# Moving the low parts of the directly read blocks of S from VectorE to GpSimd in a graph-and-experts kernel

## The chip, the core and the metric

The kernel runs on one core of one Trainium2 chip. The metric is the device time of one execution in microseconds. In the profile PE is TensorE's matmul, PEld its weight load, DVE VectorE, ACT ScalarE, POOL GpSimd, and SP SyncE, which issues most of the transfers.

## The reference

Input are `x` (8, 2048, 128), an adjacency matrix `adj` (2048, 2048) and the weights. All is float32.

```
# graph layer
HW    = layernorm(x) @ W
A     = relu((adj + adj.T) / 2);  d = rowsum(A) ** -0.5
x1    = x + relu((I - d A d) @ HW)            # S is the matrix of this product
# mixture of 8 experts, top 2 of each token
t     = layernorm(x1)
gates = normalised top 2 of softmax(t @ router_w.T)
out   = x1 + t + sum over e of gates[e] * (gelu(t @ w1[e] + b1[e]) @ w2[e] + b2[e])
```

## The kernel before, in words

**The matrix.** S is symmetric, and the scale d on both sides is put into the other operand and into the result. So the kernel keeps only one triangle of 128x128 blocks, 136 of them, in the tile `s_tri`. To be exact enough each operand of a matmul is split into a high part (rounded to fp32r) and a low part (the rest), and a product takes three matmuls: high by high, high by low and low by high (lines 969, 970, 971).

**Units.** The batches go in two halves of four. A half has 16 units, one for each block of 128 nodes, and a unit is 16 steps of three 128x512 matmuls into one PSUM bank. Units 0 to 15 (the first half) go from node block 15 down to 0, units 16 to 31 from 0 up to 15. For unit u of the first half the column of S for node block n = 15 - u is made ready in one of two `stage` tiles, high and low parts side by side. Its blocks n to 15, u + 1 of them, are read straight from the triangle: `high_direct` (ACT, line 432) copies them, `low_direct` (line 437) subtracts the copy. The other n blocks have to be turned on PE, in groups of four, into PSUM: `turn_group` (line 446), `high_group` (ACT, line 453), `low_group` (DVE, line 460). The second half loads the columns back from memory, where SP's `store_stage` (line 858) has put them; the triangle's place is then taken by `y1`, the second half's operand.

**One iteration.** The loops of all engines in the graph stage run over the same u. While PE multiplies unit u, the others finish unit u - 1 and make the stage of unit u + 1. The order on each engine is written out by hand:
- PE: 16 steps of unit u. Before the first it waits for the stage's low parts. Between the steps it does the turns, at step 4 `route(u - 2)` (line 919, the router's product, which waits for `z_lo_done`), at steps 6 and 9 the two projections of x for the second half (line 342, units 8 to 15 only), at step 12 `turn_z(u - 1)` (line 906).
- ACT: `evict(u - 1)` (line 984, it starts when unit u - 1 has left PE), `high_direct(u + 1)`, then copies and groups, `copy_z(u - 1)` (line 991).
- DVE: `mid(u - 1)` (lines 1065 to 1075: residual, statistics, `var_eps`), `low_direct(u + 1)`, then in four slots the low groups, `scale` of the two projections (line 367, each waits for its projection), in two units of four a part of the routing (`pick` in u = 5, 9, 13, from line 1087; `share` in u = 6, 10, 14, from line 1129), and `low` of the two projections (line 379). Then the statistics of the next two x tiles (line 284, which wait for their transfer), `diagonal(u + 2)` (line 422) and `z_low(u - 1)` (line 1079).
- POOL: `finish_unit(u - 1)`: `rstd` by a power (line 1033, it waits for `var_eps`), z in four pieces (line 1038), the residual `res` (line 1043). For u = 7 to 14 then the power for the next two projections (line 296) and their scale (line 316).
- SP: `store_stage(u)`, the load of the residual's x, the loads of two x tiles (line 270), `store_unit(u - 1)`, which waits for `res` and for `z_low(u - 1)`.

After unit 31 the experts follow: 256 rounds of up and down products on PE, with GELU on ACT and the gates on DVE.

One semaphore, `lo_made`, counts all low parts, direct and turned, in the order in which DVE makes them; `ops_before` and `ops_with` translate a unit or a group into that count.

Of the kernel before, what the change touches and what calls it, by code (L numbers as in the profile page):

```python
# [4 lines left out]
FP32 = mybir.dt.float32  # L5
FP32R = mybir.dt.float32r
ALU = mybir.AluOpType
# [222 lines left out]
def project_program(nc, sem, v):  # L230
# [3 lines left out]
    Q, CW, MB = v.Q, v.CW, v.MB  # L234
# [123 lines left out]
    def scale(dve, k):  # L358

        _, m = place(k)  # L360
        staged = MB - 1 - (128 - 8 * m) // 17
        dve.wait_ge(v.st.hi_made, v.st.ops_before[staged + 1])
        dve.wait_ge(v.st.s_turned, v.st.groups_before[staged + 1])
        dve.wait_ge(v.st.lo_made, v.st.ops_before[staged + 1])
        dve.wait_ge(hw_done, k + 1)
        dve.wait_ge(y_scale_done, m + 1)
        dve.tensor_tensor(out=v.y1_whole[m][:, :].rearrange("p (q f) -> p q f", f=P),
                          in0=ps_p[k][:, :].rearrange("p (q f) -> p q f", f=P),
                          in1=v.y_scale[:, m, :, None].to_broadcast([P, Q, P]), op=ALU.mult).then_inc(y1_made, 1)
# [18 lines left out]
def stage_program(nc, sem, v):  # L388


    MB, Q = v.MB, v.Q
    ps_t = [v.banks[2], v.banks[3]]
    st = Plan()
    diag_done = sem("diag_done")
    st.s_turned = s_turned = sem("s_turned")
    st.hi_made = hi_made = sem("hi_made")
    st.lo_made = lo_made = sem("lo_made")
    st.acc_done = sem("acc_done")
    st.stage_out = [sem(f"stage_out{i}") for i in range(2)]

    def column(u):
        return MB - 1 - u

    def n_groups(u):
        return (column(u) + Q - 1) // Q

    st.groups_before = [sum(n_groups(i) for i in range(u)) for u in range(MB + 1)]
    st.ops_before = [u + st.groups_before[u] for u in range(MB + 1)]

    ops_with = [st.ops_before[u] + 2 + g for u in range(MB) for g in range(n_groups(u))]  # L410

    def direct(u):
        n = column(u)
        if n < 8:
            return v.s_tri[:, 17 * n:16 * n + 16, :]
        return v.s_tri[:, 17 * n - 120:16 * 15 + n - 120 + 1:16, :]

    def diagonal(dve, u):
        n = column(u)
        dve.wait_ge(v.deg_step, v.deg_steps_until(n))  # L420
        b = block(n, n)
        dve.scalar_tensor_tensor(out=v.s_tri[:, b, :], in0=v.ident[:, :], scalar=v.deg_neg[:, n:n + 1],
                                 in1=v.s_tri[:, b, :], op0=ALU.mult, op1=ALU.add).then_inc(diag_done, 1)

    def high_direct(act, u):
        n = column(u)
        act.wait_ge(diag_done, u + 1)
        if u == 1:
            act.wait_ge(v.summed, v.all_groups)
        wait(act, st.acc_done, u - 1)  # L430
        wait(act, st.stage_out[u % 2], 16 * (u // 2))
        act.activation(v.stage[u % 2][:, 0, n:MB, :], direct(u), ACT.Copy).then_inc(hi_made, 1)

    def low_direct(dve, u):
        n = column(u)
        dve.wait_ge(hi_made, st.ops_before[u] + 1)
        dve.tensor_tensor(out=v.stage[u % 2][:, 1, n:MB, :], in0=direct(u),
                          in1=v.stage[u % 2][:, 0, n:MB, :].bitcast(FP32), op=ALU.subtract).then_inc(lo_made, 1)

    def turn_group(pe, u, g):  # L440
        n, G = column(u), st.groups_before[u] + g
        if G >= 2:
            pe.wait_ge(lo_made, ops_with[G - 2])
        for m in range(Q * g, min(Q * g + Q, n)):
            i = m - Q * g
            last = pe.transpose(ps_t[G % 2][:, i * P:(i + 1) * P], v.s_tri[:, block(n, m), :], v.ident[:, :])  # L446
        last.then_inc(s_turned, 1)

    def high_group(act, u, g):
        n, G = column(u), st.groups_before[u] + g  # L450
        a, b = Q * g, min(Q * g + Q, n)
        act.wait_ge(s_turned, G + 1)
        act.activation(v.stage[u % 2][:, 0, a:b, :].rearrange("p m f -> p (m f)"), ps_t[G % 2][:, 0:(b - a) * P],
                       ACT.Copy).then_inc(hi_made, 1)

    def low_group(dve, u, g):
        n, G = column(u), st.groups_before[u] + g
        a, b = Q * g, min(Q * g + Q, n)
        dve.wait_ge(hi_made, ops_with[G])
        dve.tensor_tensor(out=v.stage[u % 2][:, 1, a:b, :].rearrange("p m f -> p (m f)"),  # L460
                          in0=ps_t[G % 2][:, 0:(b - a) * P],
                          in1=v.stage[u % 2][:, 0, a:b, :].rearrange("p m f -> p (m f)").bitcast(FP32),
                          op=ALU.subtract).then_inc(lo_made, 1)

    st.n_groups, st.diagonal, st.high_direct, st.low_direct = n_groups, diagonal, high_direct, low_direct
    st.turn_group, st.high_group, st.low_group = turn_group, high_group, low_group
    return st

# [315 lines left out]
def graph_stage(nc, sem, v):  # L784
    B, E, MB, CW, Q, U, T = v.B, v.E, v.MB, v.CW, v.Q, v.U, v.T
    ident, pr, st = v.ident, v.pr, v.st
# [47 lines left out]
    def jobs(u):  # L834
        return [MB + 2 * (u - 8), MB + 2 * (u - 8) + 1] if 8 <= u < MB else []
# [18 lines left out]

    def sync(sp):
        def store_stage(u):
            sp.wait_ge(st.lo_made, st.ops_before[u + 1])
            sp.dma_start(v.s_dram[node_block(u)], v.stage[u % 2][:, :, :, :].bitcast(FP32)).then_inc(st.stage_out[u % 2], 16)

        def load_stage(n):  # L860
            s = (n + 1) % 2
            sp.wait_ge(acc_done, MB + n - 1)
            if n == 2:
                for i in range(2):
                    sp.wait_ge(st.stage_out[i], 16 * 7)
            sp.dma_start(v.stage[s][:, :, :, :].bitcast(FP32), v.s_dram[n]).then_inc(stage_in[s], 16)

        def load_x(u):
            wait(sp, x1_done, u)
            sp.dma_start(v.x_res[:, :, :], v.x_units[half(u), node_block(u)]).then_inc(x_res_in, 16)  # L870

        def store_unit(u):
            sp.wait_ge(res_done, u + 1)
            sp.dma_start(v.res_dram[unit(u)], v.res[:, :, :].rearrange("p q f -> p (q f)")).then_inc(res_out[half(u)], 16)
            sp.wait_ge(z_hi_done, u + 1)
            sp.wait_ge(z_lo_done, u + 1)
            sp.dma_start(v.z_dram[unit(u)], v.z_hl[:, :, :].bitcast(FP32)).then_inc(z_out[half(u)], 16)

        v.store_unit, v.store_gates = store_unit, store_gates
        sp.wait_ge(v.summed, v.all_groups)  # L880
        for u in range(U):
            if MB < u + 1 < U and node_block(u + 1) >= 2:
                load_stage(node_block(u + 1))
            if u < MB - 2:
                store_stage(u)
            load_x(u)
            for k in jobs(u + 1):
                pr.load(sp, k)
            if u == MB + 4:
                sp.wait_ge(acc_done, MB)  # L890
                v.load_weights(sp)
            if u == MB + 7:
                v.place_b2_low(sp)
            if u >= 7 and u % 4 == 3:
                store_gates(sp, (u - 7) // 4)
            if u == U - 2:
                v.load_first(sp)
            if u:
                store_unit(u - 1)

    def tensor(pe):
# [47 lines left out]
        for u in range(U):  # L949
            h = half(u)  # L950
            if h == 0:
                s = u % 2
                pe.wait_ge(st.lo_made, st.ops_before[u + 1])
                order = range(MB - 1, -1, -1)
            else:
                s = (u + 1) % 2
                if node_block(u) >= 2:
                    pe.wait_ge(stage_in[s], 16 * (node_block(u) // 2))
                order = range(MB)
            wait(pe, evicted, u - 1)  # L960
            out = acc[u % 2]
# [68 lines left out]
    def gpsimd(pool):  # L1030
# [16 lines left out]
        for u in range(U):  # L1047
            if u:
                finish_unit(u - 1)
            if jobs(u + 1):  # L1050
                pr.invert(pool, jobs(u + 1))
                for k in jobs(u + 1):
                    pr.scale_by_d(pool, k)
            if u == MB + 4:
                pool.wait_ge(acc_done, MB)
                v.zero_rows(pool)
            if u == MB + 5:
                v.weights_low(pool)
        finish_unit(U - 1)

    def vector(dve):
# [110 lines left out]
        def share(batch):  # L1172
# [7 lines left out]
                          op=ALU.subtract).then_inc(router_lo, 1)  # L1180
        for u in range(U):
            ahead = u + 1 < MB
            ks = jobs(u)
            if u:
                mid(u - 1)
            if ahead and u:
                st.low_direct(dve, u + 1)
            for g in range(4):
                if u and ahead and g < st.n_groups(u + 1):
                    st.low_group(dve, u + 1, g)  # L1190
# [317 lines left out]
```

## Time and profile before

| | |
|---|---|
| median of 3 runs | 901.16 us (900.66, 901.16, 905.78) |
| profiled execution | 904.51 us, of which span 902.8 us |
| PE, PEld busy | 854.5 us, 712.1 us |
| DVE busy | 637.2 us |
| ACT busy | 479.7 us |
| POOL busy | 297.9 us |
| granted clock of TensorE, mean | 0.983 of full speed |

The span is cut by the stages so: setup to about 87 us, the first half's units from there to about 324 us (unit 8 is reached at 193 us), the second half's units to about 520 us, and the experts. In a list of instructions each line gives start and duration in us, the engine, the line of the kernel, the operation with what it writes and reads, the shapes and how many were merged into the line, and in square brackets how long the engine had been idle before it and which engine, tile and line released it.

### The profile page before, as it was taken

How to read it: one execution, taken by the hardware profiler on the slowest of the kernel's cores; microseconds unless marked ns; L12 is line 12 of the kernel's file. 1: busy time of each engine (PE TensorE's matmuls, PEld its weight loads, DVE VectorE, ACT ScalarE, POOL GpSimd, SP SyncE). 2: the span in 40 equal slices, each digit the busy share in tenths (PEclk: the TensorE clock that was granted, in tenths of full speed). 3: DMA queues.
4: the chain of work that ended last, by engine and by line, in shares of the span. 5: the costliest groups of instructions: out<-in, count | busy, mean ns of one | idle time of the engine just before them, and what ended most of it. 6: DMA issues, size and time to landing. Idle time of an engine off the chain costs nothing.

```text
span 902.8 us, 14486 instructions
## 1 busy us (share of the span) xinstructions
PE 854.5 (95%) x4146; PEld 712.1 (79%) x4146; DVE 637.2 (71%) x1552; ACT 479.7 (53%) x872; POOL 297.9 (33%) x312
## 2 busy tenths in 40 slices
PE   4788999999899899999999999999999999999996
PEld 3688788888777788878888776888888888888884
DVE  3676644757867735262626388999999999999995
ACT  2686423233333211111011378888888888888885
POOL 1794243563564544574444440010000000000001
PEclk9896999999999999999999999999999999999999
DMA  9993366685675337877777856667777777777771
GB/s 287 315 308 122 122 261 234 227 291 191 208 260 194 111 113 264 313 258 287 278 286 267 311 219 262 260 259 284 280 268 271 275 282 274 273 272 281 283 283 46
DMA packets 93006, 222.98 MB, mean 247 GB/s; under 512 B 8888, under 2 KB 59600, under 8 KB 81056
## 3 DMA queue, kind: packets, MB, share of 16 engines
q1 hardware_dynamic: 87760, 212.96, 66.4%
q0 software_dynamic: 2688, 8.59, 2.4%
q10 hardware_dynamic: 2512, 0.86, 0.4%
q8 instruction: 23, 0.38, 0.2%
q14 instruction: 23, 0.19, 0.1%
HBM read 157.89 MB, written 64.49 MB: 246 GB/s over the span
## 4 chain that ended last, share of the span: by engine, by line
PE 69%; issue 9%; POOL 9%; DVE 6%; DMA 3%; ACT 2%; DVEq 0%; SPq 0%; ACTq 0%; POOLq 0%
PE bank L969 8%; PE bank L971 8%; PE bank L970 8%; PE bank L1379 6%; PE bank L1363 6%; PE bank L1365 6%; PE bank L1364 6%; PE bank L1376 6%; PE bank L1377 6%; POOL z L1038 5%; PE bank L342 3%; DMA x_raw<-in_x 2%; POOL rstd L1033 2%; PE bank L446 2%; PE bank L1385 1%
## 5 line engine op out<-in xcount | busy, mean ns | idle before, releaser
L1415 ACT ACTIVATE act_h<-bank,b_sb 128x512 f32<-128x512 f32 x256 | 176.6, 690 | 48.1 <-PE bank L1365 44.9
L1453 DVE TENSOR_TENSOR gated<-c_all,act_h 128x512 f32<-128x512 f32 x256 | 176.5, 690 | 30.8 <-ACT act_h L1415 25.0
L1458 DVE TENSOR_TENSOR g_lo<-gated,g_hi 128x512 fp32r<-128x512 f32 x256 | 175.7, 686 | 0.2
L1422 ACT ACTIVATE g_hi<-gated 128x512 fp32r<-128x512 f32 x256 | 159.4, 623 | 4.5 <-DVE gated L1453 4.5
L1346 POOL DMA_DIRECT2D out<-fin x32 | 24.3, 760 | 344.3 <-DVE fin L1466 333.2
L1038 POOL TENSOR_SCALAR z<-x,mv,rstd 128x128 f32<-128x128 f32 x128 | 106.4, 846 | 3.4
L969 PE MATMUL bank<-y_hi,stage 128*128 128x512 f32 x256 | 105.7, 413 | 0.7 <-DVE y_lo L743 0.7
L1363 PE MATMUL bank<-z_e,w_hi 128*128 128x512 f32 x256 | 102.8, 402 | 2.5 <-ACT act_h L1415 2.5
L991 ACT ACTIVATE z_hl<-bank 128x512 fp32r<-128x512 f32 x32 | 19.1, 598 | 157.2 <-PE bank L906 157.2
L1379 PE MATMUL bank<-g_lo,w_hi 128*128 128x512 f32 x256 | 100.9, 394 | 1.4 <-DVE g_lo L1458 1.3
L971 PE MATMUL bank<-y_hi,stage 128*128 128x512 f32 x256 | 101.4, 396 | 0.0
L969 PE MATMUL bank<-y,stage 128*128 128x512 f32 x256 | 101.2, 395 | 0.0
L1033 POOL TENSOR_TENSOR rstd<-var_eps,neg_half 128x4 f32<-128x4 f32 x32 | 48.8, 1526 | 158.5 <-DVE var_eps L1075 158.5
L970 PE MATMUL bank<-y_lo,stage 128*128 128x512 f32 x256 | 101.0, 394 | 0.0
L1376 PE MATMUL bank<-g_hi,w_lo 128*128 128x512 f32 x256 | 100.0, 391 | 0.0
L1365 PE MATMUL bank<-z_e,w_lo 128*128 128x512 f32 x256 | 99.9, 390 | 0.0
L971 PE MATMUL bank<-y,stage 128*128 128x512 f32 x256 | 99.9, 390 | 0.0
L1364 PE MATMUL bank<-z_e,w_hi 128*128 128x512 f32 x256 | 99.8, 390 | 0.0
L1377 PE MATMUL bank<-g_hi,w_hi 128*128 128x512 f32 x256 | 99.7, 389 | 0.0
L970 PE MATMUL bank<-y,stage 128*128 128x512 f32 x256 | 99.7, 389 | 0.0
L1079 DVE TENSOR_TENSOR z_hl<-bank,z_hl 128x512 fp32r<-128x512 f32 x32 | 22.0, 688 | 72.3 <-ACT z_hl L991 72.3
L1379 PEld LDWEIGHTS bank<-g_lo,w_hi 128*128 128x128 f32 x256 | 48.0, 188 | 14.9 <-DVE g_lo L1458 5.1
(128 smaller groups left out, 1481.9 us busy)
## 6 DMA issues: line engine op xcount, KB each, us to landing
c_all<-c_scratch SPq DMA_DIRECT2D x64, 1024.0 KB, 8.2
s_scratch<-stage SPq DMA_DIRECT2D x14, 2048.0 KB, 8.5
stage<-s_scratch SPq DMA_DIRECT2D x14, 2048.0 KB, 7.8
z_e<-z_scratch SPq DMA_DIRECT2D x32, 512.0 KB, 7.0
z_scratch<-z_hl SPq DMA_DIRECT2D x31, 512.0 KB, 2.7
x_raw<-in_x SPq DMA_DIRECT2D x32, 256.0 KB, 7.7
x_res<-in_x SPq DMA_DIRECT2D x32, 256.0 KB, 7.1
r_e<-res_scratch SPq DMA_DIRECT2D x32, 256.0 KB, 2.7
```

The source lines that it names most:

```text
L969: pe.matmul(out[:, :], s_hi, y_hi, start=(i == 0), stop=False)
L970: pe.matmul(out[:, :], s_hi, y_lo, start=False, stop=False)
L971: last = pe.matmul(out[:, :], s_lo, y_hi, start=False, stop=(i == MB - 1))
L1363: pe.matmul(ps_h[k][:, :], v.w1_hi[:, e, :], v.z_e[s][:, 0, :], start=True, stop=False)
L1364: pe.matmul(ps_h[k][:, :], v.w1_hi[:, e, :], v.z_e[s][:, 1, :], start=False, stop=False)
L1365: pe.matmul(ps_h[k][:, :], v.w1_lo[:, e, :], v.z_e[s][:, 0, :], start=False, stop=True).then_inc(h_done, 1)
L1376: pe.matmul(ps_o[s][:, :], v.w2_lo[:, e, :], hi[:, :], start=False, stop=False)
L1379: pe.matmul(ps_o[s][:, :], v.w2_hi[:, e, :], lo[:, :], start=False, stop=(e == E - 1)).then_inc(o_done, 1)
L1415: act.activation(v.act_h[e % R][:, :], ps_h[e % 2][:, :], ACT.Gelu, bias=v.b1_sb[:, e:e + 1]).then_inc(gelu_done, 1)
L1422: act.activation(v.g_hi[e % R][:, :], v.gated[e % R][:, :], ACT.Copy).then_inc(hi_done, 1)
L1453: dve.tensor_tensor(out=v.gated[e % R][:, :], in0=v.c_all[s][:, e, :], in1=v.act_h[e % R][:, :], op=ALU.mult).then_inc(gated_done, 1)
L1458: dve.tensor_tensor(out=v.g_lo[e % R][:, :], in0=v.gated[e % R][:, :], in1=v.g_hi[e % R][:, :].bitcast(FP32), op=ALU.subtract).then_inc(lo ...
```

## The change

`low_direct` of units 2 to 15 is taken off DVE's list in the graph stage and put on POOL's, behind `finish_unit(u - 1)` and ahead of the power for the projections. Those of units 0 and 1 stay on DVE in the setup. The direct low parts get a semaphore of their own, `direct_lo`, and `lo_made` now counts the turned groups alone; PE, SP and DVE wait for both where they waited for one.

```diff
-        dve.wait_ge(v.st.lo_made, v.st.ops_before[staged + 1])
+        dve.wait_ge(v.st.direct_lo, staged + 1)
+        dve.wait_ge(v.st.lo_made, v.st.groups_before[staged + 1])
...
-    def low_direct(dve, u):
+    def low_direct(eng, u):
         n = column(u)
-        dve.wait_ge(hi_made, st.ops_before[u] + 1)
-        dve.tensor_tensor(out=v.stage[u % 2][:, 1, n:MB, :], in0=direct(u),
-                          in1=v.stage[u % 2][:, 0, n:MB, :].bitcast(FP32), op=ALU.subtract).then_inc(lo_made, 1)
+        eng.wait_ge(hi_made, st.ops_before[u] + 1)
+        eng.tensor_tensor(out=v.stage[u % 2][:, 1, n:MB, :], in0=direct(u),
+                          in1=v.stage[u % 2][:, 0, n:MB, :].bitcast(FP32), op=ALU.subtract).then_inc(direct_lo, 1)
...
         if G >= 2:
-            pe.wait_ge(lo_made, ops_with[G - 2])
+            pe.wait_ge(lo_made, G - 1)
...
         def store_stage(u):
-            sp.wait_ge(st.lo_made, st.ops_before[u + 1])
+            sp.wait_ge(st.direct_lo, u + 1)
+            sp.wait_ge(st.lo_made, st.groups_before[u + 1])
...
             if h == 0:
                 s = u % 2
-                pe.wait_ge(st.lo_made, st.ops_before[u + 1])
+                pe.wait_ge(st.direct_lo, u + 1)
+                pe.wait_ge(st.lo_made, st.groups_before[u + 1])
...
         for u in range(U):                       # POOL
             if u:
                 finish_unit(u - 1)
+            if u and u + 1 < MB:
+                st.low_direct(pool, u + 1)
             if jobs(u + 1):
                 pr.invert(pool, jobs(u + 1))
...
             if u:                                # DVE
                 mid(u - 1)
-            if ahead and u:
-                st.low_direct(dve, u + 1)
             for g in range(4):
```

## Rows read from the trace of the kernel before

**Rows 1.** From the page: busy time, share and instructions of each engine.

```profile
PE 854.5 (95%) x4146; PEld 712.1 (79%) x4146; DVE 637.2 (71%) x1552; ACT 479.7 (53%) x872; POOL 297.9 (33%) x312
```

**Rows 2.** PE's waits, 100 to 330 us: waiter, releaser, us in total, times, longest.

```profile
PE bank L919 <- issue: 4.8, 2, 3.0
PE bank L919 <- DVE z_hl L1079: 3.6, 3, 1.4
```

**Rows 3.** DVE's instructions in order of time, iterations 9 to 14.

```profile
219.43 0.29 DVE L1089 TENSOR_TENSOR logits<-gate_parts 128x128 f32<-128x128 f32 x1
...
235.26 0.69 DVE L367 TENSOR_TENSOR y_whole<-bank,y_scale 128x512 f32<-128x512 f32 x1 [1.70 <-PE bank L342]
...
236.41 0.28 DVE L1134 TENSOR_TENSOR picked<-expo,same 128x128 f32<-128x128 f32 x1
...
237.04 0.86 DVE L1142 SCALAR_TENSOR_TENSOR guarded<-sum_all,sum_top 128x16 f32<-128x16 f32 x1
...
257.66 0.87 DVE L284 BATCH_NORM_STATS2 x_stats<-x_raw 128x6 f32<-128x128 f32 x4 [3.79 <-DMA x_raw<-in_x]
...
268.85 1.56 DVE L379 TENSOR_TENSOR y<-y_whole,y 128x512 fp32r<-128x512 f32 x2
272.22 0.87 DVE L284 BATCH_NORM_STATS2 x_stats<-x_raw 128x6 f32<-128x128 f32 x4 [1.81 <-DMA x_raw<-in_x]
...
275.65 0.69 DVE L1079 TENSOR_TENSOR z_hl<-bank,z_hl 128x512 fp32r<-128x512 f32 x1
...
284.72 0.29 DVE L1089 TENSOR_TENSOR logits<-gate_parts 128x128 f32<-128x128 f32 x1
...
285.37 0.93 DVE L1106 TENSOR_TENSOR shifted<-logits,top 128x128 f32<-128x128 f32 x1
...
303.39 1.10 DVE L1129 TENSOR_TENSOR same<-is_1st,is_2nd 128x128 f32<-128x128 f32 x1
```

**Rows 4.** All direct low parts of DVE: count, ns least/median/most, first and last start.

```profile
L437 DVE TENSOR_TENSOR stage<-s_tri,stage x16: 292/1285/2282, 76.0 to 296.5; 128x128 fp32r<-128x128 f32 x1, 128x256 fp32r<-128x256 f32 x1, 128x384 fp32r<-128x384 f32 x1, 128x512 fp32r<-128x512 f32 x1
```

**Rows 5.** POOL's instructions in order of time, iterations 9, 10, 12, 13, 14 and 16.

```profile
211.11 2.34 POOL L1033 TENSOR_TENSOR rstd<-var_eps,neg_half 128x4 f32<-128x4 f32 x1 [0.63 <-DVE var_eps L1075]
...
230.78 2.47 POOL L1033 TENSOR_TENSOR rstd<-var_eps,neg_half 128x4 f32<-128x4 f32 x1 [0.62 <-DVE var_eps L1075]
...
236.58 1.28 POOL L1043 TENSOR_TENSOR res<-x,z 128x512 f32<-128x512 f32 x1
...
263.72 2.74 POOL L1033 TENSOR_TENSOR rstd<-var_eps,neg_half 128x4 f32<-128x4 f32 x1 [0.62 <-DVE var_eps L1075]
...
278.58 2.87 POOL L1033 TENSOR_TENSOR rstd<-var_eps,neg_half 128x4 f32<-128x4 f32 x1 [0.62 <-DVE var_eps L1075]
...
296.72 3.00 POOL L1033 TENSOR_TENSOR rstd<-var_eps,neg_half 128x4 f32<-128x4 f32 x1 [0.62 <-DVE var_eps L1075]
...
326.93 1.03 POOL L1033 TENSOR_TENSOR rstd<-var_eps,neg_half 128x4 f32<-128x4 f32 x1 [7.00 <-DVE var_eps L1075]
```

**Rows 6.** POOL's two-operand instructions in the setup, by form: busy, mean ns, idle before.

```profile
L573 POOL TENSOR_TENSOR col_sum<-col_sum,s_tri 128x1024 f32<-128x1024 f32 x6 | 14.2, 2368 | 2.0 <-ACT s_tri L608 2.0
...
L573 POOL TENSOR_TENSOR col_sum<-col_sum,s_tri 128x640 f32<-128x640 f32 x2 | 3.1, 1548 | 0.0
```

**Rows 7.** A long POOL instruction and DVE beside it, iteration 21.

```profile
393.82 5.21 POOL L1275 TENSOR_TENSOR w_lo<-w_raw,w_hi 128x1024 fp32r<-128x1024 f32 x2 [2.09 <-ACT w_hi L1262]
...
395.49 1.29 DVE L1065 TENSOR_TENSOR x<-x,x_res 128x512 f32<-128x512 f32 x1 [2.09 <-ACT x L984]
```

**Rows 8.** ACT and PE in iteration 13: unit 12 has left PE; the router's product.

```profile
273.73 0.69 ACT L984 ACTIVATE x<-bank,d_out 128x512 f32<-128x512 f32 x1 [2.17 <-PE bank L971]
...
276.83 0.40 PE L919 MATMUL bank<-z_hl,router 128*128 128x512 f32 x1
```

**Rows 9.** Two stretches after PE's long waits: busy times, then PEclk, DMA share, GB/s.

```profile
230.00:235.00 5.00, 5.00 (x34) 4.48 (x33) 3.45 (x9) 1.66 (x3) 4.26 (x5) 1.00 1.12 427
...
295.00:299.00 4.00, 4.00 (x17) 3.45 (x16) 3.68 (x11) 1.30 (x2) 3.27 (x4) 0.57 0.87 262
```

More of the change, by code:

```diff
@@ L396, in stage_program @@
     st.hi_made = hi_made = sem("hi_made")
+    st.direct_lo = direct_lo = sem("direct_lo")
     st.lo_made = lo_made = sem("lo_made")
```

## The prediction

> **What bounds the kernel now.** I read the page first. PE is busy for 95% of the span [rows 1], so the change can gain only where PE stands still, and loses wherever it makes PE stand longer. Next come PE's own waits in the first half. All but one of those that matter are in front of one instruction, the router's product at step 4 of iterations 10, 11, 12, 14 and 15: 4.8 us in two waits and 3.6 us in three, 8.4 us together [rows 2]. It waits for `z_low`, the last thing on DVE's list of the iteration before. So DVE's list sets the pace from iteration 9 on, though DVE is idle 29% of the span. In the order of time one sees what the list itself waits for: for the second projection (1.70 us idle in iteration 10), and in iterations 11 and 12 for the x tiles' transfer (3.79 and 1.81 us); in 10, 13 and 14, which carry a routing part, it runs from the second `scale` to `z_low` with no such wait [rows 3]. Anything put into that last stretch reaches PE in full.
>
> **What is removed.** 14 subtractions of DVE, up to 2282 ns each [rows 4]. They stand between `var_eps` and the first `scale`. The second `scale` waits for a projection that PE reaches at step 9, whatever DVE did before, and DVE already idles 1.70 us there [rows 3]. So taking the 1.75 us subtraction away in iteration 10 makes that wait longer and nothing earlier. I take a gain of 0 on DVE; the cover is PE's five steps from `route` to the second projection. POOL does gain: its power `rstd` takes 1.03 us alone, and 2.34 to 3.00 us where DVE's subtraction runs beside it [rows 5]. z comes 1.3 to 2 us sooner; PE hardly waits for z, so this is worth 0 too. But it decides where the new instruction lands.
>
> **What is added.** A two-operand POOL instruction takes 2368 ns for 1024 elements and 1548 ns for 640 [rows 6], so 2.14 ns an element and 0.18 us besides, 0.273 us a block: 3.2 us for unit 10 (11 blocks), 3.5, 3.7, 4.0, 4.3 and 4.55 us for unit 15 (16 blocks), about twice DVE's own. It starts behind `res`. In iteration 10 the power ends at 230.78 + 2.47 = 233.25 and `res` at 237.86, 4.61 us later; with the power at 1.03 us, `res` ends 1.03 + 4.61 = 5.64 us after the power's start and the new instruction begins 0.06 us later, so at start + 5.70.
>
> Is it late for PE? In iteration 12 it is there from 263.72 + 5.70 = 269.42 to about 273.9 (with one short hold by DVE), and unit 12 leaves PE at 273.73 [rows 5, 8]. Unit 13 would begin about 0.2 us late, and the wait at `route` swallows that. The others come out earlier or as close. What is queued behind it on POOL, the next power, waits for x statistics that end later still: 0. SP stores the stage only after `z_low`, later than that: 0. The added waits of PE, SP and DVE are on counts already reached: 0. Units 2 to 8 have small subtractions and a DVE with slack: 0.
>
> **The port.** Here is the real cost. `L1142`, 16 elements wide, starts at 237.04 beside POOL's `res` and takes 0.86 us: it ends at 237.90, and `res` at 237.86 [rows 3, 5]. `L1106` takes 0.93 us and `L1129` 1.10 us beside a `res`, where `L1089` on the same shape takes 0.29 [rows 3]. Beside a longer one, `w_lo` of 2.6 us, a residual addition of 512 elements takes 1.29 us, where `L367` of that size takes 0.69: it gets in only between the two instructions [rows 3, 7]. So a DVE instruction with two operands in SBUF stands until POOL's ends, also when POOL's is long. The Trainium skill says the same (SBUF — State Buffer, section Who interferes with whom: a DVE instruction with two SBUF inputs and a GpSimd one that reads SBUF exclude each other, for the whole instruction). By it the sum below stands; without it only the first rival's 0 to 3 us would be left.
>
> **The sum**, in the times of before (what comes later shifts as a whole). Iteration 9: the new instruction runs from 211.11 + 5.70 = 216.8 to 220.0; `L1089` wants to start at 219.43 and ends 0.7 us later than before. Iteration 10: DVE's `L1129`, waiting since before `res` ended, is let in first, then the new instruction runs from about 236.6 to 240.1. `L1134` (236.41, end 236.69) now ends at 240.2, which is +3.5; the 0.7 us that `L1142` loses to `res` is saved: +2.8. Iteration 11: the pair `L379` is held, but 3.79 us of idle time behind it cover that: +0.1. Iteration 12: of the pair at 268.85 the second is held until 273.9 and ends at 274.45, 2.2 us past the 272.22 at which the statistics began; these had a second wait of 0.2 us inside, so 2.0 remain. `z_low` ended at 276.34 and `route` began at 276.83, so PE loses 1.5, but POOL and DVE 2.0, and the next iteration's hold hangs on POOL: +2.0. Iteration 13: 278.58 + 5.70 + 4.3 = 288.6; `L1089` (284.72) ends 3.75 us later; `L1106` saves 0.64: +3.1. Iteration 14: 296.72 + 5.70 + 4.55 = 307.0; `L1129` ended at 304.49, now at 307.1: +2.6 [rows 3, 5, 8].
>
> That is 11.3 us. Then the clock. After PE's wait of 3.0 us the granted clock is 0.57 over 4 us, close to the lower of its two levels (1.2 GHz), which costs 0.43 x 4 = 1.7 us; after the other long wait, 1.8 us, it is 1.00 [rows 2, 9]. The waits in iterations 11 and 15 grow past 3 us (1.2 on average, plus 2.8 and 2.6). In 11 the transfer's wait covers the loss. In 15 nothing does: +1.7. Sum 13.0 us. The profiled execution would go from 904.5 to 917.5 us. It lies 0.4% above the median of the runs shown; from 901.2 the forecast is **914 us**.
>
> Bounds. POOL's price in the form with an fp32r output is 5.21 / 2 = 2.6 us per 1024 at most, against 2.37 [rows 6, 7]; 10% on the six is +2 us. Further clock drops in iterations 10 and 13 cost at most 1.7 us each: 919 to 920. Below: if DVE's second `L379` slips in ahead of POOL in iteration 12, that iteration costs 0.8 at most, and if the clock does not drop in 15, 1.7 less: 911.
>
> **Rivals.**
> *The port hardly counts* (DVE gets in between pieces of POOL's long instruction). For it: no row shows a POOL instruction of 4 us with DVE beside it. Against: the 2.6 us one held DVE. Then only lateness at the unit starts and a power of 1.03 us remain: 901 to 904 us. Chance 0.18.
> *The gain on DVE counts.* Of the six subtractions 11.7 us (1.62 to 2.28) leave DVE; if `z_low` followed that, PE's 8.4 us of waits would go and with them the clock drop of 1.7: 891 us. It decides if the second `scale` is not held by PE, and the 1.70 us idle says it is. Chance 0.08.
> *POOL becomes the bound at the unit starts.* If the subtraction takes 10 to 15% more and DVE's short instructions get in ahead of it, units 12 to 15 start 0.5 to 1.2 us late each, and longer PE waits drop the clock after four units: 914 + 4 + 2 x 1.7 = 921 us and up to 925. Chance 0.12.
> The forecast has 0.62.
>
> **How the numbers follow.** 1%, 9 us, is about what a measurement of this kernel can tell from no change. Faster by more: 0.07, nearly all of the second rival. Within 1%: the first rival, a bit of the second, and the part of the forecast's own case in which the holds are shorter (below 910): 0.25. Slower: 0.68. The forecast's own range is 909 to 919. To leave out no more than 2 in 10 it must reach the first rival's upper part and the third's middle: 903 to 921.
>
> **What would show it.** Right: L437 on POOL with 3.2 to 4.6 us in iterations 9 to 14; `L1089` or `L1129` and `L1134` in 10, 13 and 14 with durations of 3 to 4 us, ending with it; `rstd` near 1.03 us; PE's waits at the router's product up from 8.4 to near 20 us; and low clock behind two or more of them. Wrong: short durations of those DVE instructions; a second `scale` that starts sooner; PE waiting at line 969 for POOL.

## The result: 916.8 us, 1.6% slower

The changed kernel took 916.83 us in the median of four runs (916.57 to 917.65), the kernel before 901.62 in four. The ratio is 1.0158, 95% interval 1.0128 to 1.0188. The profiled execution took 917.65 us with a span of 916.0, which is 13.2 us over the span of before. The forecast was 914 on the median and +13.0 in the profiled execution.

### The profile page after: what moved, and what is told of

It is laid out like the page before. It is cut to its first block, busy times and chain, and to the rows that moved or that the text cites. A ratio compares the mean times of both kernels' runs of the same rounds, so it can differ in the third digit from the quotient of the medians.

```text
span 916.0 us, 14517 instructions
## 1 busy us (share of the span) xinstructions
PE 856.8 (94%) x4146; PEld 712.0 (78%) x4146; DVE 637.4 (70%) x1538; ACT 479.1 (52%) x872; POOL 320.9 (35%) x326
## 4 chain that ended last, share of the span: by engine, by line
PE 66%; issue 10%; POOL 9%; DVE 8%; ACT 4%; DMA 2%; DVEq 0%; SPq 0%; ACTq 0%; POOLq 0%
PE bank L973 7%; PE bank L975 7%; PE bank L974 7%; PE bank L1383 5%; PE bank L1367 5%; PE bank L1369 5%; PE bank L1368 5%; PE bank L1380 5%; PE bank L1381 5%; POOL z L1042 5%; PE bank L342 3%; PE bank L448 2%; POOL res L1047 2%; ACT s_tri L610 1%; PE bank L1389 1%
## 5 line engine op out<-in xcount | busy, mean ns | idle before, releaser
L1037 POOL TENSOR_TENSOR rstd<-var_eps,neg_half 128x4 f32<-128x4 f32 x32 | 33.4, 1043 | 153.5 <-DVE var_eps L1081 153.5
```

## The profile after

Lines of the kernel have moved: 437 is 439, 919 is 922, 969 is 973, 1033 is 1037, 1079 is 1085, 1089 is 1095, 1129 is 1135, 379 is 380. In the experiments they move by a few more; the tile's name tells which instruction is meant. First the page's line of busy times, against [rows 1].

```profile
PE 856.8 (94%) x4146; PEld 712.0 (78%) x4146; DVE 637.4 (70%) x1538; ACT 479.1 (52%) x872; POOL 320.9 (35%) x326
```

DVE has 14 instructions fewer and is as busy as before. The work that left it came back as waiting: an instruction held by POOL counts as busy from its start. So a share of busy time does not show this loss. PE's waits of the first half (100 to 345 us) do, against [rows 2].

```profile
PE bank L922 <- issue: 8.3, 2, 5.5
PE bank L922 <- DVE z_hl L1085: 8.0, 4, 4.0
PE bank L973 <- POOL stage L439: 1.4, 3, 0.6
```

The waits at the router's product have gone from 8.4 to 16.3 us. POOL's own lateness at the start of a unit costs PE 1.4 us in three waits. Next POOL in order of time, against [rows 5].

```profile
211.32 1.04 POOL L1037 TENSOR_TENSOR rstd<-var_eps,neg_half 128x4 f32<-128x4 f32 x1 [0.63 <-DVE var_eps L1081]
...
216.93 3.22 POOL L439 TENSOR_TENSOR stage<-s_tri,stage 128x1408 fp32r<-128x1408 f32 x1
...
236.96 3.50 POOL L439 TENSOR_TENSOR stage<-s_tri,stage 128x1536 fp32r<-128x1536 f32 x1
...
272.64 4.48 POOL L439 TENSOR_TENSOR stage<-s_tri,stage 128x1792 fp32r<-128x1792 f32 x1
...
289.26 4.34 POOL L439 TENSOR_TENSOR stage<-s_tri,stage 128x1920 fp32r<-128x1920 f32 x1
...
310.40 4.61 POOL L439 TENSOR_TENSOR stage<-s_tri,stage 128x2048 fp32r<-128x2048 f32 x1
```

The power takes 1.04 us where it took 2.34, and the subtraction what the setup's sums had told: 3.2, 3.5, 4.0, 4.3 and 4.55 expected. The one of 1792 elements has some wait inside. DVE in order of time, against [rows 3]: the instructions that were held, and all of `z_low` from iteration 8 to 14.

```profile
208.39 0.68 DVE L1085 TENSOR_TENSOR z_hl<-bank,z_hl 128x512 fp32r<-128x512 f32 x1
...
219.06 1.24 DVE L1095 TENSOR_TENSOR logits<-gate_parts 128x128 f32<-128x128 f32 x1
...
228.43 0.68 DVE L1085 TENSOR_TENSOR z_hl<-bank,z_hl 128x512 fp32r<-128x512 f32 x1
...
237.43 0.69 DVE L368 TENSOR_TENSOR y_whole<-bank,y_scale 128x512 f32<-128x512 f32 x1 [2.93 <-PE bank L342]
238.04 2.58 DVE L1135 TENSOR_TENSOR same<-is_1st,is_2nd 128x128 f32<-128x128 f32 x1
...
247.74 0.68 DVE L1085 TENSOR_TENSOR z_hl<-bank,z_hl 128x512 fp32r<-128x512 f32 x1
...
255.80 5.26 DVE L380 TENSOR_TENSOR y<-y_whole,y 128x512 fp32r<-128x512 f32 x2
...
264.10 0.68 DVE L1085 TENSOR_TENSOR z_hl<-bank,z_hl 128x512 fp32r<-128x512 f32 x1
...
272.14 5.54 DVE L380 TENSOR_TENSOR y<-y_whole,y 128x512 fp32r<-128x512 f32 x2
...
280.71 0.68 DVE L1085 TENSOR_TENSOR z_hl<-bank,z_hl 128x512 fp32r<-128x512 f32 x1
...
289.51 4.23 DVE L1095 TENSOR_TENSOR logits<-gate_parts 128x128 f32<-128x128 f32 x1
...
301.88 0.68 DVE L1085 TENSOR_TENSOR z_hl<-bank,z_hl 128x512 fp32r<-128x512 f32 x1
...
311.23 3.93 DVE L1135 TENSOR_TENSOR same<-is_1st,is_2nd 128x128 f32<-128x128 f32 x1
...
322.01 0.68 DVE L1085 TENSOR_TENSOR z_hl<-bank,z_hl 128x512 fp32r<-128x512 f32 x1
```

An instruction of 128 elements takes 4.23 us. It starts at 289.51, 0.25 us behind POOL's, and ends at 293.74; POOL's ends at 293.60. The same 0.29 us instruction was [rows 3]'s line at 284.72. The starts of `z_low` give the account by iteration:

| iteration | before | after | lag | gained in it | forecast |
|---|---|---|---|---|---|
| 8 | 208.17 | 208.39 | 0.22 | | |
| 9 | 227.85 | 228.43 | 0.58 | +0.4 | +0.7 |
| 10 | 244.34 | 247.74 | 3.40 | +2.8 | +2.8 |
| 11 | 260.79 | 264.10 | 3.31 | -0.1 | +0.1 |
| 12 | 275.65 | 280.71 | 5.06 | +1.8 | +2.0 |
| 13 | 293.79 | 301.88 | 8.09 | +3.0 | +3.1 |
| 14 | 311.35 | 322.01 | 10.66 | +2.6 | +2.6 |

Last PE and ACT: three stretches of the changed kernel behind PE's waits of 2.83, 5.50 and 4.00 us (iterations 10, 14, 15), against [rows 9], and the moment at which unit 15 has left PE.

```profile
229.20:235.00 5.80, 5.79 (x24) 5.14 (x25) 3.22 (x12) 2.52 (x5) 4.96 (x8) 0.71 0.89 362
...
302.60:308.00 5.40, 5.34 (x24) 4.58 (x25) 2.67 (x11) 2.33 (x4) 4.57 (x7) 0.72 0.67 197
322.80:328.00 5.20, 5.16 (x22) 4.42 (x23) 2.37 (x11) 0.22 (x1) 4.63 (x7) 0.68 0.58 189
```

```profile
336.02 0.69 ACT L988 ACTIVATE x<-bank,d_out 128x512 f32<-128x512 f32 x1 [2.17 <-PE bank L975]
```

The same eviction was at 323.88 before: 12.1 us of lag, 1.5 more than `z_low` had in iteration 14. The low clock of iteration 15, (1 - 0.68) x 5.2 = 1.7 us, accounts for that. The lag stays at 12.1 us through the second half. The last 1.0 us comes in the experts, 0.7 of it in one step where PE waits 0.5 us for the load of `z_e`; nothing ties it to the change.

## The experiments

Each ratio is to the kernel before, timed together with that run; absolute times of different experiments compare less well.

**e1 and e2: early units alone, late units alone.**

```diff
-            if u and u + 1 < MB:                 # e1
+            if u and u + 1 <= 8:
                 st.low_direct(pool, u + 1)
...
+            if ahead and u + 1 >= 9:
+                dve.wait_ge(st.direct_lo, u + 1)
+                st.low_direct(dve, u + 1)
...
-            if u and u + 1 < MB:                 # e2
+            if u + 1 >= 10 and u + 1 < MB:
                 st.low_direct(pool, u + 1)
...
+            if u and u + 1 <= 9:
+                st.low_direct(dve, u + 1)
```

> Only the direct low parts of units 2 to 8 are on POOL, those of 9 to 15 are back on DVE. Port theory (a long POOL subtraction holds DVE's two-operand instructions, `z_low` comes late, PE waits for it at the router's product): in iterations 1 to 7 DVE has slack before `z_low`, so 901 to 903 us, no change from before. If the added waits or the second count cost something, or POOL's lateness in general, part of the 15 us stays: 904 to 908.

> Only units 10 to 15 are on POOL (iterations 9 to 14), units 2 to 9 are back on DVE. Port theory: all of the loss is here, 914 to 917 us. A loss spread over all units by their size (133 blocks, 81 of them in these six) would give 61% of it: 910 to 911.

e1: 903.17 us against 903.88, ratio 0.9996 (0.9981 to 1.0010). e2: 917.94 us, ratio 1.0160 (1.0127 to 1.0193). All of the loss that shows lies in the six late iterations. The second count with its waits, and POOL's work in the early units, cost nothing that can be told from 0. A loss that follows the blocks handled would have shown 1.0096 in e2.

**e3: POOL's instruction cut to one block.**

```diff
+        end = MB if u < 2 else n + 1
...
-        eng.tensor_tensor(out=v.stage[u % 2][:, 1, n:MB, :], in0=direct(u),
+        eng.tensor_tensor(out=v.stage[u % 2][:, 1, n:end, :], in0=direct(u)[:, 0:end - n, :],
...
```

> As the change, but POOL's subtraction covers only the first block (0.46 us); the other direct low parts are left out. Nothing is on DVE in their place. Port theory with no gain on DVE: the holds fall to 0.3 us, PE's waits at the router's product go back to about 8 us: 900 to 903 us. If DVE's relief is worth something once POOL is out of the way: 891 to 897.

900.95 us, ratio 0.9978 (0.9957 to 1.0000). With the order of the change but without its length the loss is gone. And this bounds DVE's relief: taking all 14 subtractions off DVE, with POOL out of the way, is worth 2 us, with 0 to 4 in the interval, and not 10. PE's waits at the router's product are those of before:

```profile
PE bank L923 <- issue: 4.3, 2, 2.4
PE bank L923 <- DVE z_hl L1086: 3.3, 3, 1.6
```

The second `scale` of iteration 10 shows where the relief goes:

```profile
231.74 0.69 DVE L368 TENSOR_TENSOR y_whole<-bank,y_scale 128x512 f32<-128x512 f32 x1 [2.72 <-PE bank L342]
```

It starts 7.40 us after the iteration's `z_low` began (224.34), and in the kernel before 7.41 us after (227.85 to 235.26) [rows 3]. The 1.75 us that DVE no longer spends became idle time, 1.0 us here and 0.55 us in front of the first `scale`.

**e4: a subtraction that nobody waits for, added to the kernel before.**

```diff
...
+            if u and u + 1 < MB:
+                k = min(u + 2, 11)
+                each = v.ident[:, None, :].to_broadcast([P, k, P])
+                pool.tensor_tensor(out=v.spare[:, 0:k, :], in0=each, in1=each, op=ALU.subtract)
```

> The kernel before, with DVE's subtraction where it was, and beside it a POOL subtraction of constants into unused memory behind `finish_unit`, of u + 2 blocks at most 11 (3.2 us); no instruction waits for it. Port theory: it starts 1.3 to 2 us later than in the changed kernel, behind the slower power, and then holds DVE in iteration 9 for 1.7 us, in 10 for 2.7, in 13 and 14 for 3 each, in 11 and 12 for nothing: 10 us and a clock drop or two, 911 to 914 us. If the loss is POOL's lateness for PE: 901 to 902, since nothing waits for this one.

915.73 us against 903.88, ratio 1.0133 (1.0102 to 1.0164). That is 12 us, what was expected (10 us and a clock drop or two), though the absolute time lies above the range given. Nothing waits for this instruction, yet it costs most of what the change cost. So the cost of the change is for the most part not when POOL's result comes, but what POOL keeps from DVE meanwhile. POOL and DVE of iteration 13:

```profile
293.61 2.59 POOL L1054 TENSOR_TENSOR spare<-ident 128x1408 fp32r<-128x1408 f32 x1
```

```profile
293.73 2.62 DVE L1113 TENSOR_TENSOR same<-logits,top 128x128 f32<-128x128 f32 x1
```

Both end within 0.15 us of each other. My durations were off: this form takes 2.6 us and not 3.2, so the holds are shorter. From iteration 8 to 14 `z_low` falls back by 9.2 us against the kernel before (210.99 to 323.33, there 208.17 to 311.35). Behind PE's waits (15.8 us together) the clock is low in four iterations, with a mean of 0.72 over 6 us in three of them.

**e5 and e6: `z_low` ahead of the x statistics**, in the kernel before and in the changed one.

```diff
+            if u:
+                z_low(u - 1)
             for k in jobs(u + 1):
                 pr.statistics(dve, k)
             if u + 2 < MB:
                 st.diagonal(dve, u + 2)
-            if u:
-                z_low(u - 1)
```

> The kernel before with `z_low` ahead of the x statistics and the diagonal on DVE's list, nothing else. If z_low's place at the end of the list is what hands DVE's lateness to PE, PE's 8 us at the router's product go, and the 1.7 us of low clock behind them; part comes back as waits at other places (for z at step 12, for the x tiles' transfer): 893 to 897 us. If PE's wait only moves: 900 to 904.

> The changed kernel with the same edit. The port theory says that POOL's holds of 3 to 4 us lie ahead of `z_low` in either order, so they still make it late, but 3 us of statistics no longer come on top: PE waits where hold is longer than that, about 2 us each in iterations 13 and 14 and the starts of units 12 to 14 are late by 0.5 us each: 900 to 906 us. If the 15 us came from something else than z_low's lateness, 912 or more.

e5: 904.06 us, ratio 1.0020 (1.0005 to 1.0035). e6: 919.57 us, ratio 1.0189 (1.0164 to 1.0215). Both expectations failed. PE's waits of e5, 100 to 345 us:

```profile
PE bank L342 <- ACT x_t L329: 6.9, 3, 3.4
```

and of e6:

```profile
PE bank L342 <- ACT x_t L329: 11.6, 5, 3.4
```

In e5 the wait at the router's product is gone and stands at step 6; in e6 most of it has moved there. `diagonal` is still behind the statistics; ACT's `high_direct` waits for it, and on ACT the x copy that the projection needs is queued behind `high_direct`. So DVE's list hands its lateness to PE over two roads of about the same length. My reading of [rows 2] as the one place was too narrow: a wait that shows in a profile hides the one right behind it.

**e7: POOL's subtraction in pieces of two blocks**, in the changed kernel.

```diff
+        step = MB if u < 2 else 2
+        for a in range(n, MB, step):
+            b = min(a + step, MB)
+            last = eng.tensor_tensor(out=v.stage[u % 2][:, 1, a:b, :], in0=direct(u)[:, a - n:b - n, :],
+                                     in1=v.stage[u % 2][:, 0, a:b, :].bitcast(FP32), op=ALU.subtract)
+        last.then_inc(direct_lo, 1)
```

> The changed kernel with POOL's subtraction cut into instructions of two blocks (0.73 us each, so 5.8 to 6.5 us for unit 15). Port theory: each DVE instruction with two operands is held by one piece, 0.7 us at most, but six or seven of them follow each other in a routing part, and POOL is at it longer, so the sum of holds is much the same and the units' starts get later by 1 to 2 us: 914 to 922 us. If it is the length of one hold that counts: 903 to 907.

911.02 us, ratio 1.0092 (1.0067 to 1.0117): neither of the two. I had thought that DVE would lose its turn at each piece. POOL and DVE of iteration 13:

```profile
285.84 5.53 POOL L442 TENSOR_TENSOR stage<-s_tri,stage 128x256 fp32r<-128x256 f32 x8
```

```profile
287.92 0.88 DVE L1099 TENSOR_TENSOR logits<-gate_parts 128x128 f32<-128x128 f32 x1
...
289.16 0.39 DVE L1116 TENSOR_TENSOR shifted<-logits,top 128x128 f32<-128x128 f32 x1
289.47 0.82 DVE L1118 TENSOR_TENSOR same<-logits,top 128x128 f32<-128x128 f32 x1
290.33 0.72 DVE L1124 TENSOR_TENSOR key<-same,rev_iota 128x128 f32<-128x128 f32 x1
```

Each takes 0.29 us alone, so the four lose 0.59, 0.10, 0.53 and 0.43 us, 1.7 us in all against 3.9 for the whole instruction, although POOL is busy 1.2 us longer. DVE gets in between pieces, and the reductions among its instructions (one operand, `TENSOR_REDUCE`) keep their 0.29 us beside them. Not every instruction with one operand does: the cast of 128 elements takes 0.23 us alone, 0.65 us beside a piece here (240.34), and in e10 1.19 us (237.59) beside `res`, ending 0.08 us after it. The price is at the starts of the units, where PE now waits up to 1.6 us for POOL.

**e8: early units on POOL, and `z_low` first.**

> POOL makes the direct low parts of units 2 to 8 alone, and `z_low` goes ahead of the statistics. By the port theory POOL's part is free in the early units and worth nothing either: the same as the kernel before with that edit alone, within 1.5 us. A candidate for the fastest version.

904.78 us, ratio 1.0021 (0.9999 to 1.0043), the same as e5, as expected.

**e9, e10 and e11: `z_low` and `diagonal` both ahead of the statistics**, in the kernel before, the changed one and the one in pieces.

```diff
+            if u + 2 < MB:
+                st.diagonal(dve, u + 2)
+            if u:
+                z_low(u - 1)
             for k in jobs(u + 1):
                 pr.statistics(dve, k)
...
```

> The kernel before with both `z_low` and `diagonal` ahead of the x statistics on DVE's list. Theory after the last runs: DVE's lateness reaches PE over two roads, `z_low` to the router's product and `diagonal` to ACT's `high_direct`, behind which the x copy for the projection waits; moving one alone only moved the wait. With both out of the way the next one in line is `y1_made` (second projection at step 9), with some 1 to 2 us of wait in three iterations: 894 to 898 us. If the loop of DVE's list, mid to mid over the x tiles' transfer, is the bound by itself: 900 to 904.

> The changed kernel with the same edit. DVE's holds by POOL stay (4 us in iterations 13 and 14), so its list is still the longer, but only the starts of units 12 to 14 and `y1_made` hand it on: 900 to 908 us. If DVE's lateness reaches PE whatever the order: 914 or more.

> POOL's subtraction in pieces of two blocks, with both moved. The pieces alone gave 911 us against 917: DVE's instructions wait for a piece of 0.7 us and not for 4 us. With the roads to PE cleared as well, and DVE 2 us shorter by the subtraction that it no longer makes: 896 to 902 us; PE then waits for POOL at the starts of units 12 to 15, 1 to 1.6 us each.

e9: 902.19 us, ratio 0.9993 (0.9974 to 1.0012), no gain. e10: 911.51 us, ratio 1.0109 (1.0088 to 1.0131), some 4 us better than the change as it was made, but not the 900 to 908 us expected. e11: 911.80 us, ratio 1.0102 (1.0080 to 1.0125), far from the 896 to 902 us expected. PE's waits, 100 to 345 us, in e9, then in e10 and then in e11:

```profile
PE bank L342 <- DVE y_whole L367: 5.6, 3, 2.8
```

```profile
PE bank L973 <- POOL stage L439: 5.8, 4, 2.5
PE bank L922 <- issue: 4.2, 2, 2.7
PE bank L909 <- POOL z L1042: 2.7, 3, 1.1
PE bank L342 <- DVE y_whole L368: 1.7, 3, 0.8
```

```profile
PE bank L977 <- POOL stage L442: 8.5, 3, 4.5
```

With both roads cleared, e9 waits on a third: the first `scale`, which stands behind `mid` and the direct subtraction. Here that subtraction is on the path, and in e10, where POOL has it, the wait is 1.7 us and not 5.6. But PE now waits for POOL at the units' starts, and for z. In e11 POOL is longer at its pieces, and these waits reach 3.1 us at unit 11 and 4.5 us at unit 15, where I had expected 1 to 1.6 us; so with both moved the pieces are worth nothing over the whole instruction. The rival "POOL becomes the bound at the unit starts" is what one meets once `z_low` and `diagonal` are out of the way.

**e12: the subtraction on DVE, between the two `scale`s**, where DVE stood idle, with both moved as in e9.

```diff
-            if u and u + 1 < MB:
-                st.low_direct(pool, u + 1)
...
+            if ahead and u and not ks:
+                st.low_direct(dve, u + 1)
...
                 if ks and g < 2:
                     pr.scale(dve, ks[g])
+                if ks and ahead and g == 0:
+                    st.low_direct(dve, u + 1)
...
```

> No subtraction on POOL. With both moved, DVE makes the direct low part between the first and the second `scale`, where it stood idle 1.7 to 2.7 us for the projection (the count of its own allows that order). Nothing is held and the first `scale` comes 2 us sooner: 890 to 896 us, the fastest version; not under the other with both moved if that wait was not on the path.

898.43 us (897.46 to 899.93), ratio 0.9966 (0.9950 to 0.9983): faster than the kernel before and the changed one, though not the 890 to 896 us expected. e9 differs from it in the subtraction's place alone and took 902.19 us beside it. DVE of iteration 10, and PE's largest waits:

```profile
231.17 0.68 DVE L368 TENSOR_TENSOR y_whole<-bank,y_scale 128x512 f32<-128x512 f32 x1
231.76 1.75 DVE L439 TENSOR_TENSOR stage<-s_tri,stage 128x1536 fp32r<-128x1536 f32 x1
233.43 0.68 DVE L368 TENSOR_TENSOR y_whole<-bank,y_scale 128x512 f32<-128x512 f32 x1
```

```profile
PE bank L909 <- POOL z L1042: 3.6, 2, 2.0
PE bank L342 <- DVE y_whole L368: 0.8, 1, 0.8
```

The subtraction fills what was 1.70 us of idle time in [rows 3], and `y_whole` costs PE 0.8 us where it cost 5.6 in e9. POOL's power again starts beside no DVE subtraction. What is left is the wait for z.

## Why the prediction was right, step by step

**What bounds.** That DVE's list paces the late iterations held: e4 lengthened that list by an instruction on POOL for whose result nothing waits. That its last entry, `z_low`, is the place was half of it: e5 and e9 show `diagonal` and the first `scale` close behind. The forecast did not hang on it, since each of the three shifts with the list.

**What is removed is worth 0.** e3 gives 2 us, 0 to 4 in the interval. The rival of a gain on DVE (891 us) needed the second `scale` to be free of PE. In e3 it starts at the same distance from `z_low` as before, to 0.01 us, with 2.72 us of idle time in front of it in place of 1.70. (The changed kernel's 2.93 us are not that clear, since its clock was low there.)

**POOL's price** was right to 0.1 us for 11, 12, 15 and 16 blocks. For 13 and 14 the instruction itself was held by the first of the `L380` pair, so units 12 to 14 began 0.3 to 0.6 us late where I had 0.2; the wait at the router's product shrank by as much.

**The port.** The losses by iteration came as forecast, to 0.1 us in iterations 10, 13 and 14, 0.2 in 11 and 0.3 in 9 and 12. The Trainium skill's rule (SBUF — State Buffer, section Who interferes with whom) is what the trace shows: an instruction with two SBUF operands waits to the end of POOL's, 4.23 us in the longest case. It is not what the trace shows for POOL's power (last section). In iteration 10 the way was another: I had let `L1129` in first and held `L1134`. In the trace PE's clock had dropped, the second `scale` came 1.6 us later against the rest, and `L1135` (the former `L1129`) was held from 238.04. It ends when POOL's does, either way, which is why the sum agreed.

**The clock.** The 1.7 us in iteration 15 was right. The drop behind the 2.83 us wait in iteration 10 was in the bounds, not in the sum; it added nothing to the lag of `z_low`, since it only moved DVE into a hold that would have ended at the same time. I had counted on a low clock in iteration 11, free too; PE's wait there was 2.60 us and the clock stayed at 1.00. The sign "near 20 us" of waits at the router's product was missed with 16.3: 1.4 us stood at the starts of units, and in iteration 10 PE ran 1.7 us longer at the low clock ((1 - 0.71) x 5.8) instead of waiting.

**The 13.2 us** are then 10.4 from the six iterations, 1.5 from the clock, 0.2 from before iteration 9 and 1.0 in the experts that the forecast did not have; its own sum was 11.3 + 1.7. That the total agreed to 0.2 us is in part luck. Against the medians the ratio gives 14 us, 12 to 17.

## What to carry to other kernels

The subtraction moved from DVE to POOL took twice as long (4.61 us against 2.28 for 16 blocks) and during all of it shut out DVE's instructions with two SBUF operands. Before moving such an instruction, list those that follow on DVE at that time and ask whether DVE's list is on the path there. If it must go to POOL, try it in pieces: they cost less than the whole here (911 against 917 us), but no less once PE waited for POOL itself (e11 against e10). And an instruction may be free where it stands: look for the idle time in DVE's own list (e12) before looking for another engine.

## What was not expected of the hardware

- The length of PE's wait alone does not tell whether the clock falls behind it. It fell after 2.83 us in the changed kernel, and stayed after 2.60 us there. It fell after 3.0 us in the kernel before, to 0.57 over 4 us [rows 9], and stayed at 1.00 after 3.11 us in e1. PE's wait and the stretch around it, e1:

```profile
289.63 0.47 PE L922 MATMUL bank<-z_hl,router 128*128 128x512 f32 x1 [3.11 <-issue]
```

```profile
288.00:293.00 5.00, 3.37 (x21) 3.01 (x22) 4.75 (x19) 2.40 (x2) 3.46 (x4) 1.00 0.51 154
```

In e6 the clock was 0.72 over 6 us behind a wait of 2.99 us (iteration 10) and stayed at 1.00 behind one of 3.04 us (iteration 11). So a term for the clock is worth 1.7 us, and near 3 us no run here shows what decides it.
- The runs of the kernel before spread from 896.6 to 907.5 us. Part of such a spread is there before the first unit, in a setup that no experiment touched: the first matmul of unit 0 starts at 83.2 us in the profile of e1, 83.3 in e3, 86.5 in the changed kernel, 87.0 in the kernel before and 88.6 in e4. So compare distances within the stage (as from `z_low` to `z_low`) rather than spans of single executions. What makes the setup differ was not looked into, nor what part the clock has.
- A power on a few elements does not hold DVE as a subtraction does: `L1065` (512 elements, two SBUF operands) takes its usual 0.68 us at 208.77 in the kernel before, inside POOL's power of 8 elements that runs from 208.14 for 1.66 us. The other way round the power does wait: 2.34 to 3.00 us beside DVE's subtraction and 1.03 without [rows 5].
